# A two-block transformer kernel: stage two written out without loops, its maxima and next-block work spread through the attention, values of two key tiles in four 32-column products, softmax sums added by GpSimd

## What is computed

```python
def reference(x, ctx_4096, ...):
    ...
    # first block
    x = x + _L0_xattn_ref(_layernorm(x), ctx_4096, Wq_d, W_qk, Wkv_d, Wv_u)
    x = x + _L0_ffn_ref(_layernorm(x), weight_q, scale, zero_point, bias)
    # second block
    x = x + _L1_xattn_ref(_layernorm(x), ctx_4096, Wq, Wk, Wv, Wo)
    x = x + _L1_ffn_ref(_layernorm(x), W, b, A, Bmat, LiMEs)

def _L0_xattn_ref(Q, K, Wq_d, W_qk, Wkv_d, Wv_u):      # 16 heads of 32
    C_q = Q @ Wq_d                                      # 64 wide
    C_kv = K @ Wkv_d                                    # 32 wide, shared by all heads
    CqWqk = (C_q @ W_qk).reshape(b, n, H, LKV)
    scores = jnp.einsum('bnhl,bkl->bhnk', CqWqk, C_kv) / jnp.sqrt(LKV)
    attn = jax.nn.softmax(scores, axis=-1)
    V_up = (C_kv @ Wv_u).reshape(b, nkv, H, HD)
    out = jnp.einsum('bhnk,bkhd->bnhd', attn, V_up)
    return out.reshape(b, n, H * HD)
```

## Time and profile before

| | us |
|---|---|
| median of 3 runs | 2154.68 (2154.64 to 2156.42) |
| the profiled execution, its own time | 2159.22 |
| its span, first to last instruction | 2157.4 |
| stage one, in that span | 0 to 291 |
| stage two | 291 to 1099 |
| stages three and four | 1099 to 2157 |
| PE busy in the span | 1956.8 (91%) |
| DVE, ACT, POOL busy | 1132.7, 941.3, 650.4 |

### The profile page before, as it was taken

The page is one execution under the profiler, slowest core; times in us unless marked ns, Lnnn a source line. Parts: engine busy times, 40 slices in busy tenths (PEclk is TensorE's granted clock), DMA queues, the critical chain, the costliest instruction groups (busy, mean ns, idle before and its releaser), DMA issues. The chain is left out here.

```text
span 2157.4 us, 25080 instructions
## 1 busy us (share of the span) xinstructions
PE 1956.8 (91%) x8690; PEld 1366.7 (63%) x8690; DVE 1132.7 (53%) x2097; ACT 941.3 (44%) x1614; POOL 650.4 (30%) x504
## 2 busy tenths in 40 slices
PE   7999959988996997899669999999999999999986
PEld 7999944437444743743536777766776777766762
DVE  2434316645654664564355666665556566564413
ACT  2323212441451344145126566655666466665550
POOL 0000000000000000000017676665666566765650
PEclk9999976998997998899769999999999999999985
DMA  5457640002000200200161222212322222211112
GB/s 177 156 176 240 182 105 1 1 16 76 27 0 25 93 0 15 76 18 1 59 175 42 71 67 71 58 42 68 81 71 71 51 80 71 55 48 53 30 30 92
DMA packets 109692, 149.38 MB, mean 69 GB/s; under 512 B 28777, under 2 KB 87529, under 8 KB 106510
## 3 DMA queue, kind: packets, MB, share of 16 engines
q1 hardware_dynamic: 101326, 143.79, 23.2%
q10 hardware_dynamic: 8256, 4.22, 0.8%
HBM read 96.52 MB, written 51.39 MB: 69 GB/s over the span
## 5 line engine op out<-in xcount | busy, mean ns | idle before, releaser
L1405 POOL TENSOR_TENSOR pl<-pf,ph 128x512 fp32r<-128x512 f32 (+1 forms) x480 | 639.9, 1352 | 349.9 <-ACT pf L1572 348.0
L1568 ACT ACTIVATE ph<-ps 128x512 fp32r<-128x512 f32 (+1 forms) x480 | 287.4, 599 | 350.4 <-PE ps L1476 349.7
L1631 DVE TENSOR_REDUCE pm<-ps 128x1 f32<-128x464 f32 (+1 forms) x512 | 321.1, 637 | 156.7 <-PE ps L1422 148.1
L1103 DVE TENSOR_REDUCE pm<-ps 128x1 f32<-128x400 f32 (+1 forms) x512 | 268.9, 569 | 140.4 <-PE ps L816 136.9
L1020 ACT ACTIVATE pr<-ps 128x1024 f32<-128x1024 f32 (+1 forms) x208 | 211.3, 1023 | 211.1 <-PE ps L834 210.7
L1572 ACT ACTIVATE pf<-ps 128x512 f32<-128x512 f32 (+1 forms) x480 | 287.2, 598 | 2.4 <-POOL pl L1405 2.1
L1394 POOL MEMSET vf<- 128x96 f32 x1 | 0.2, 183 | 788.0 <-POOLq L612 788.0
L849 PE MATMUL ps<-pr,cv 128*64 128x512 f32 (+1 forms) x832 | 226.3, 619 | 7.6 <-ACT pr L1020 7.5
L1422 PE MATMUL ps<-kh,qh 96*128 96x464 f32 (+1 forms) x512 | 203.4, 404 | 20.7 <-DMA ql<-q_scr 12.6
L1494 PE MATMUL ps<-pl,vh 128*97 128x512 f32 (+1 forms) x480 | 195.1, 406 | 20.8 <-POOL pl L1405 19.7
L1491 PE MATMUL ps<-ph,vh 128*97 128x512 f32 (+1 forms) x480 | 195.7, 408 | 4.8 <-ACT ph L1568 4.8
(11 more groups left out here) (215 smaller groups left out, 2662.0 us busy)
## 6 DMA issues: line engine op xcount, KB each, us to landing
woT<-wo_turned SPq DMA_DIRECT2D x16, 1536.0 KB, 8.8
cnat<-in_ctx_dram SPq DMA_DIRECT2D x16, 768.0 KB
q_scr<-qst SPq DMA_DIRECT2D x48, 256.0 KB, 2.3
kf<-k_scr SPq DMA_DIRECT2D x16, 696.4 KB, 4.9
vf<-v_scr SPq DMA_DIRECT2D x16, 672.0 KB
v_scr<-vst SPq DMA_DIRECT2D x64, 144.0 KB, 1.9
k_scr<-kst SPq DMA_DIRECT2D x36, 192.0 KB, 5.4
wo_turned<-wo_out SPq DMA_DIRECT2D x32, 192.0 KB, 3.1
```

The costliest lines, as they stand in the source:

```text
L1103: dve.reduce_max(pm[:, j, ch:ch + 1], bank(at)[:, 0:k], AX).then_inc(mx_done, 1)
L1405: pool.tensor_tensor(pl[0:m, n % 2, cols], pf[0:m, half, :], ph[0:m, n % 2, cols].bitcast(F32), ALU.subtract).then_inc(plo, 1)
L1568: act.activation(ph[0:keys[kt], n % 2, cols], src, ACT.Exp, scale=S1).then_inc(phi, 1)
L1631: ins = dve.reduce_max(pm[:, j, ch:ch + 1], at[:, 0:cuts[ch][1]], AX)
```

## The change

Stage two is unrolled: batches and groups become one line of 16 group numbers s (`S = B * NG`), each engine follows one list made by `course(s)`, and the semaphore counts are plain numbers. These are the parts:

1. **Values in fours.** Key tiles are taken in pairs (`UNITS`: six pairs and one alone). `cv` has 32 columns. The product of key tile kt and query half h goes to partitions 32 (2 (kt mod 2) + h) and up, so the two halves of two key tiles are four products of 32 columns in a row. `wvu` has its rows four times for it. `pr` has six buffers.
2. **The sums on GpSimd.** It adds `pr` of the 13 key tiles up in `acc` (12 additions of 128x1024 a group, each waiting for the one before it). Behind the four products of a raise, eight products of 128x128 by one column of ones bring the sums over the partitions.
3. **One ring of three banks.** Maxima, turned maxima, raise, queries, turned rows, feed-forward and projections are items of one list; each waits for the read of the item three before it. Every group has 32 maxima in it (26 of the next group, 6 of the one after), and the feed-forward product, layer norms, turning, projections of the batch before and queries of the batch after lie at fixed places between them.
4. **Double buffers** for context, values and `x` of two batches.
5. **Stage one** takes over the small weight loads, the first layer norm, turning and query product of batch 0 (`x`, `cq`), has four weight buffers (`NW = 4`), and issues the dequantised weight's load later.

```diff
-    NW = 6
+    NW = 4
...
-                elif i < 2:
-
-                    pe.wait_ge(*((row_done, ONE + e * NG + g) if g > 1 else (qhi, ONE + e * NU)))
...
-                for half in range(2):
-                    mm = pe.matmul(bank(OB)[64 * half:64 * half + 64, :], cv[0:keys[kt], kt, :],
-                                   pr[0:keys[kt], n % 2, half * BANK:(half + 1) * BANK],
-                                   start=(kt == 0), stop=(kt == KT - 1))
...
+    UNITS = [(0, 1), (2, 3), (4, 5), (6, 7), (8, 9), (10, 11), (12,)]
+    NPR = 6
+    LEAD = 6
...
+        def beside(s):
+            b, g = divmod(s, NG)
+            e, f = b - 1, b + 1
+            extra, tail = {LEAD + 6: [("raise", s - 1)]} if s else {}, []
+            if g == 0 and e >= 0:
+                extra |= {25: [("xt", e, 0, 0)], 26: [("xt", e, 0, 1)], 20: [("a", b, 4)], 23: [("a", b, 5)],
+                          27: [("a", b, 6)], 30: [("a", b, 7)]}
+                tail = [("ffn", e, 0), ("ffn", e, 1)]
+            if g == 1 and e >= 0:
+                extra |= {19: [("xt", e, 1, 0)], 20: [("xt", e, 1, 1)], 24: [("q", e, 0)], 28: [("q", e, 1)]}
+                tail = [("q", e, 2)]
+            if g == 2 and e >= 0:
+                extra |= {10: [("q", e, 3)], 17: [("q", e, 4)]}
+                tail = [("q", e, 5)]
...
+        def course(s):
+            main, row, tail = beside(s)
...
+            for t in UNITS[0]:
+                yield "scores", s, t
+                yield from some(2)
+            for j, unit in enumerate(UNITS):
+                for t in UNITS[j + 1] if j + 1 < len(UNITS) else ():
+                    yield "scores", s, t
+                    yield from some(2)
+                for t in unit:
+                    yield "values", s, t
+                if j < len(UNITS) - 2:
+                    yield from some(3)
+                if j == len(UNITS) - 2:
+                    assert len(given) == len(main)
+                    yield from row
+            yield from tail
...
+            for s in range(S):
+                for kt in range(1, KT):
+                    n, m = s * KT + kt, keys[kt]
+                    if kt == 1 and s >= 2:
+                        pool.wait_ge(*turned(("raise", s - 2)))
+                    pool.wait_ge(exp_done, n + 1)
+                    old = pr[0:m, (n - 1) % NPR, :] if kt == 1 else acc[0:m, s % 2, :]
+                    if kt > 1:
+                        pool.wait_ge(added, s * (KT - 1) + kt - 1)
+                    pool.tensor_tensor(acc[0:m, s % 2, :], pr[0:m, n % NPR, :], old, ALU.add).then_inc(added, 1)
...
+                for half in range(2):
+                    r = (kt % 2 * 2 + half) * HD0
+                    mm = pe.matmul(bank(OB)[r:r + HD0, :], cv[0:keys[kt], b % 2, kt, :],
+                                   pr[0:keys[kt], n % NPR, half * BANK:(half + 1) * BANK],
+                                   start=(kt < 2), stop=(kt >= KT - 2))
...
+            def ring_item(g):
+                n, out = at[g][0], bank_of(g)
+                if n >= RB:
+                    pe.wait_ge(*read(order[n - RB]))
...
+                    pe.wait_ge(added, (g[1] + 1) * (KT - 1))
+                    for t in range(TT):
+                        for c in range(2):
+                            for h in range(2):
+                                i = TT * G * HD0 + t * G + c * 2 + h
+                                q0 = h * BANK + c * T + t * P
+                                mm = pe.matmul(out[:, i:i + 1], acc[:, g[1] % 2, q0:q0 + P], ones[:, :],
+                                               start=True, stop=True)
...
+            def probs(s, kt):
+                n = s * KT + kt
+                act.wait_ge(s_mm, n + 1)
+                if n >= NPR:
+                    s0, t0 = divmod(n - NPR, KT)
+                    act.wait_ge(av_mm, n - NPR + 1)
+                    act.wait_ge(added, s0 * (KT - 1) + max(t0, 1))
```

More of the change, by code:

```diff
@@ new lines, in items, with last_reader @@
+        def items():
+            yield from before()
+            for s in range(S):
+                yield from (w for w in course(s) if w[0] not in ("scores", "values"))
+            yield from after()
+        def last_reader(g):
+            if g[0] in ("xat", "cq") or g[0] == "q" and g[2] >= NQ or g[0] == "xt" and g[2:] == (0, 0):
+                return "act"
+            return "dve"
+        at, order, count = {}, [], {"act": 0, "dve": 0}
+        for g in items():
+            count[last_reader(g)] += g[0] != "row"
+            at[g] = (len(order), count[last_reader(g)])
+            order.append(g)
```

932 lines of the change are left out of this document (432 added, 500 removed).

## The result

The changed kernel takes 2197.54 us (median of 4 runs, 2195.36 to 2197.96) against 2155.55 us for the kernel before: 1.0187 times as long, with a 95% interval of 1.0166 to 1.0207. The forecast was 2065 us, faster. The change made the kernel 42 us slower; direction and range were wrong.

What follows compares the result with a forecast made beforehand. TensorE was taken to bound batches 1 and 2, GpSimd batch 0. Stage two falls from 733.6 to 125 + 2 x 157 + 150 + 66 = 655 us, the start gains 11.2: 2065 us, range 2025 to 2125 (some 80%).

Steps and rivals of the forecast that it cites:

- Values in fours: Stage two's value products: two key tiles cost what one did, 7.2 us less a group of heads on TensorE.
- GpSimd's addition: Stage two: 2.6 us per 128x1024 addition (bounds 2.3 to 3.4), 31.2 us a group, setting batch 0's pace at 125 us.
- TensorE's own work: Batches 1 and 2 of stage two: 141.8 us of TensorE work each, the bound; with 15 us of waits 157.
- VectorE's durations: Batches 1 and 2: maxima 79 us, layer norms 5.5 us each, VectorE some 118 us a batch in all.
- rival 2: Stage two: GpSimd's addition takes 3.4 us, 163 us for each batch, time 2128 us; chance 9%.
- The placement: Batches 1 and 2: 15.6 us of layer norm waits go, 15 us of short ring waits come; batch 145 to 172 us.
- Batch 3 and tail: End of stage two: last batch 150 us with no next batch to prepare, then a tail of 66 us.
- Start: Up to the first exponential: stage one 3 us longer, first exponential at 341.5 us, 11 us gained (bounds 333 and 348).
- Rival 1: Value products: four do not run side by side, 6.0 us a group, time 2125 us; chance 10%.
- rival 3: Stage two: less lost in the ring, 145 us a batch, 2.4 us an addition; 2014 at best, 2030 likelier; chance 15%.
- Rival 6: Stage two: layer norm waits stay as reads wait for TensorE, 15.6 us a batch, 2100 us; 10% together with rival 4.
- rival 4: Stage two: the ring costs double, 172 us a batch, time 2110 us; chance 10% together with Rival 6.

Runs made afterwards that it cites:

- small additions: Changed kernel, but GpSimd adds only 32 of the 1,024 columns of each key tile (output not the reference's): 2133.52 us, 0.9895 of before.
- ones column: Changed kernel's order and double buffers, but values as two 64-column products with the ones column among them, no GpSimd additions or one-column products: 2142.59 us.

## Why the prediction was wrong, step by step

- **Values in fours: right.** 1.00 us a block, with nothing of the 0.1 us more that the prediction gave as another estimate; the first group took 23.4 us against 23.6.
- **Ones products: right.** 1.8 us a group, from the run without them; 1.75 was taken.
- **GpSimd's addition: right in kind, 2.37 us** against 2.6 and inside 2.3 to 3.4; the estimate of 2.25 that stood beside it was nearer. Where nothing else delays them they start 2.52 us apart, 30.2 us for twelve. That GpSimd sets the pace of a plain group shows in the second (33.1 us, with TensorE waiting 3.8 us for an addition), but batch 0 took 131.6 us, not 125, since its third and fourth groups already carry a layer norm and the next batch's queries.
- **TensorE's own work: right.** 143.4 and 142.8 us in batches 1 and 2, 141.8 in the sum.
- **The step that failed first: VectorE's durations.** The prediction priced a layer norm at 5.5 us from the earlier trace rows, where GpSimd did nothing in the whole stage, and put 116 us of GpSimd work a batch beside it without asking what the two share. The stalls came to 32 us a batch, not 15; without the holds they are 19.6 (small additions). The sign was in the trace of the kernel before, in stage three, where GpSimd works beside layer norms. The same step as L79 above, from 1099 to 2100 us:

```profile
L79 DVE SCALAR_TENSOR_TENSOR ln_y<-ln_u,ln_y 128x2 f32<-128x2 f32 x9 | 7.9, 873 | 0.3
```

  873 ns on two numbers, where it is 161 when GpSimd rests. By the count used above, VectorE's excess in that stretch of the kernel before is 43.6 us. The prediction looked at how VectorE may slow GpSimd (rival 2) and not at the other direction.
- **The step that failed second: the clock had no term.** The prediction noted that the half-speed parts lie behind the waits, and then let them go with the waits. Half of 54.8 us is 27 us a batch; without any hold it is still 17 to 26 us. Nor do all falls lie behind waits: some stand right behind the one-column products, with TensorE busy throughout. Removing 16 us of work from between waits of the same total gave back 3 to 8 us (small additions against ones column). Put together for batch 1: 143.4 + 32.0 + 27.4 = 202.8 us.
- **The placement gives no idle time back.** The 15.6 us of waits for layer norms were to go, at a price of 15 us of short ones: on this point the sum was 5 to 7 us low (19.6 to 21.8 us without holds), and it counted nothing for what the same idle time does to the clock once there is less work.
- **Batch 3 and tail:** 155.6 and 74.9 us against 150 and 66. Three waits of the tail, 4.0, 6.9 and 7.0 us, are for the last additions and the two layer norms.
- **Start: wrong by 11 us.** First exponential at 352.6, not 341.5. Stage one was priced at 3 us more by its products, and no issue of a transfer on ScalarE was counted: 11 of them alone take 15.5 us, with TensorE waiting behind for 9.2. The text had named growth by over 6 us as a sign of being wrong; it was 14.
- **Rivals.** The only way to a slower kernel was an addition of over 3.5 us. It was 2.37, and the kernel is slower all the same. Rival 1 fell with the first point, rival 2 with the additions' 2.37 us; rival 3 had the additions' 2.4 us right and the ring wrong. Rival 6 did not happen as told (no wait for `xn` is left before the tail), rival 4's 172 us a batch was on the right side and far too small. Behind stage two nothing changed, as forecast (1058.5 us).

The sum of the misses, from the batches' first exponentials: +6.6 in batch 0, +45.8 and +47.6 in batches 1 and 2, +5.6 in batch 3, +8.9 in the tail, +11.1 at the start, together 125.6 us; from 2069 to the 2195.4 us of the profiled run it is 126.4.

## What to carry to other kernels

A duration read from a stage in which an engine rests does not hold once that engine gets work: look for the same instruction in a stage where both work, above all for a mean of several hundred ns on a handful of numbers. Write TensorE's time as work at full clock, idle time and what is lost at half clock; a saving on an engine that has regular waits is paid back in part by the third term, so shorten the waits first (reading one bank after each part of a layer norm was worth 15 us here, the saved products 11). And count transfers that an engine issues as its work, with who waits behind them.

## What the runs showed of the hardware

- VectorE instructions with two inputs in SBUF, and `tensor_scalar` from SBUF to SBUF on 128x512, wait while GpSimd's two-input addition runs: 0.16 us became up to 2.34 us, 0.55 us up to 2.72 us, behind additions of 2.37 us. A `tensor_scalar` on two int32 numbers a partition went from 0.17 to 1.32 us, one on a single f32 number did not. Beside running additions, reads of an accumulator bank (569 ns) stayed at their length, and so did two kinds with one input in SBUF, a maximum over 128x32 numbers (186 to 188 ns, 15 times) and `bn_stats` on 128x512 (693 to 695 ns). Behind additions of 512 columns without a pause, single instructions of 0.28 us took 7.98 and 23.7 us.
- Four products with 32 columns each, on the four column ranges of the array, take as long as two with 64: 1.00 us a block of two passes.
- About the same idle time, 20 to 22 us a batch, went with 37 to 52 us of busy time at half clock where the work was 136 to 137 us, and with 13 to 20 us where it was 159 to 163.
- VectorE's inverse of 128x512 in an accumulator bank took 3365 ns, where a subtraction or product of that size takes 690.
- Some kernels spread widely from run to run, 2119.81 to 2149.37 us and 2188.55 to 2202.50 us, where the ones-column kernel stays within 1.5 us; why was not tested. Of gains of 10.8 us and 7.4 us at the front of the program, the medians of two kernels kept 3.5 us and 0.5 us.
